# Causal scores in three tiles of PSUM instead of four, and one slice of the next latent query moved ahead of the values

## What is computed

```python
scores = einsum('bhsr,btr->bhst', q_lat, c_kv) + einsum('bhsd,btd->bhst', q_rope, k_rope[:, 0])
scores = scores / sqrt(DN + DR)
scores = where(tril(ones((s, s))), scores, finfo.min)      # s = 128, causal
probs  = softmax(scores, axis=-1)
out_lat = einsum('bhst,btr->bhsr', probs, c_kv)            # then w_uv and w_out per head
```

## Time and profile before

| | |
|---|---|
| time, median of 3 | 1919.72 us (1919.02 to 1920.83) |
| profiled execution, span | 1917.3 us |
| PE busy | 1909.2 us (100%), weight loads 1615.0 us (84%) |
| DVE, ACT, POOL busy | 1531.8 (80%), 1168.9 (61%), 1048.7 us (55%) |
| chain that ended last | PE 97%, DVE 2%, DMA 1% |
| DMA | 393.13 MB in 86473 packets, queue 58.0% of 16 engines |

### The profile page before, as it was taken

One profiled execution on the slowest core, in us unless ns is written; L12 is line 12 of the kernel. 1 busy time (PEld: TensorE's weight loads), 2 busy tenths in 40 slices (PEclk: granted clock), 3 DMA queues, 4 the chain that ended last, 5 costly groups with the idle time before them and its releaser, 6 DMA issues.

```text
span 1917.3 us, 32648 instructions
## 1 busy us (share of the span) xinstructions
PE 1909.2 (100%) x10048; PEld 1615.0 (84%) x10048; DVE 1531.8 (80%) x2655; ACT 1168.9 (61%) x2648; POOL 1048.7 (55%) x891
## 2 busy tenths in 40 slices
PE   9999999999999999999999999999999999999999
PEld 7888888888888888888888888888888877888887
DVE  6778888888888887877777777777878889996677
ACT  5456767676758575765555555555656668766441
POOL 5468777787869696865555556555565511000000
PEclk9999999999999999999999999999999999999999
DMA  9838474647474655588546264464628286466645
GB/s 361 333 105 317 133 260 130 253 125 263 122 266 138 231 171 199 195 319 328 181 151 233 77 230 132 158 207 140 217 82 302 91 285 250 198 220 245 229 152 176
DMA packets 86473, 393.13 MB, mean 205 GB/s; under 512 B 9472, under 2 KB 10240, under 8 KB 67328
## 3 DMA queue, kind: packets, MB, share of 16 engines
q1 hardware_dynamic: 86400, 392.21, 58.0%
HBM read 236.46 MB, written 155.71 MB: 205 GB/s over the span
## 4 chain that ended last, share of the span: by engine, by line
PE 97%; DVE 2%; DMA 1%; ACT 0%; issue 0%; DVEq 0%; POOL 0%; ACTq 0%; SPq 0%
PE at_out L1281 11%; PE at_out L1285 10%; PE at_out L1282 10%; PE at_qbank L55 7%; PE at_qbank L57 7%; PE at_qbank L56 7%; PE at_score L1244 6%; PE at_score L1235 3%; PE at_turned L1256 3%; PE at_qbank L1605 3%; PE at_score L1605 2%; PE at_out L1605 2%; PE at_value L56 2%; PE at_value L55 2%; PE at_value L57 2%; PE at_qbank L1608 2%
## 5 line engine op out<-in xcount | busy, mean ns | idle before, releaser
L2620 DVE TENSOR_TENSOR at_acc<-at_out,at_acc 128x512 f32<-128x512 f32 x640 | 438.9, 689 | 138.2 <-PE at_out L1285 136.2
L2266 POOL TENSOR_TENSOR at_acc<-at_stage,at_acc 128x512 f32<-128x512 f32 x256 | 332.3, 1298 | 184.1 <-ACT at_stage L1747 174.5
L1281 PE MATMUL at_out<-at_wvo,at_val_hi 128*128 128x512 f32 x896 | 365.3, 408 | 0.5 <-ACT at_stage L1747 0.2
L1285 PE MATMUL at_out<-at_wvo,at_val_lo 128*128 128x512 f32 x896 | 350.6, 391 | 0.0
L1282 PE MATMUL at_out<-at_wvo,at_val_hi 128*128 128x512 f32 x896 | 350.5, 391 | 0.0
L1747 ACT ACTIVATE at_stage<-at_out 128x512 f32<-128x512 f32 x256 | 153.0, 599 | 125.2 <-PE at_out L1285 112.9
L1787 ACT ACTIVATE at_pT_hi<-at_turned 128x512 fp32r<-128x512 f32 x128 | 76.4, 597 | 245.8 <-PE at_turned L1256 245.8
L2226 POOL TENSOR_TENSOR at_probs<-at_probs,at_row_stats 128x512 f32<-128x512 f32 x128 | 133.3, 1041 | 148.2 <-DVE at_row_stats L2582 148.2
L1781 ACT ACTIVATE at_probs<-at_probs,at_row_stats 128x128 f32<-128x128 f32 x512 | 197.7, 388 | 8.8 <-DVE at_row_stats L2577 8.8
L1285 PEld LDWEIGHTS at_out<-at_wvo,at_val_lo 128*128 128x128 f32 x896 | 168.4, 188 | 37.8
L1281 PEld LDWEIGHTS at_out<-at_wvo,at_val_hi 128*128 128x128 f32 x896 | 169.1, 189 | 31.1 <-DVE at_acc L2620 5.7
(11 more groups left out here) (313 smaller groups left out, 4772.3 us busy)
## 6 DMA issues: line engine op xcount, KB each, us to landing
parts_d<-at_rope_tmp SPq DMA_DIRECT2D x32, 1024.0 KB, 6.1
at_qrope<-parts_d SPq DMA_DIRECT2D x128, 256.0 KB, 5.3
wvo_d<-at_wvo SPq DMA_DIRECT2D x16, 2048.0 KB, 7.8
at_wvo<-wvo_d SPq DMA_DIRECT2D x16, 2048.0 KB, 8.1
ff_w_d<-ff_w SPq DMA_DIRECT2D x21, 1024.0 KB, 6.2
ff_w<-ff_w_d SPq DMA_DIRECT2D x21, 1024.0 KB, 4.8
ab_raw<-in_w_heads SPq DMA_DIRECT2D x32, 576.0 KB, 5.5
wvo_d<-at_wvo SPq DMA_DIRECT2D x16, 1024.0 KB, 9.8
```

Source lines behind the costliest of these rows:

```text
L1281: pe.matmul(out, hi, weight[:, 0], start=start, stop=False, skip_group_check=True)
L1285: pe.matmul(out, lo, weight[:, 0], start=False, stop=True, skip_group_check=True).then_inc(out_ready, 1)
L2266: pool.tensor_tensor(at, stage[group][z][:], at, ALU.add).then_inc(pool_added, 1)
L2620: dve.tensor_tensor(at, outb[FACTORS[name][2]][:], at, ALU.add).then_inc(added, 1)
```

## The change

For the 64 first queries of a square only the first 64 keys count, since the scores are causal. The changed kernel computes the 64 last queries of both heads of a batch in one tile (two heads x 64 queries on the partitions, 128 keys), one tile for each batch, and puts the first queries of both batches side by side in a third tile (64 keys for each batch). So there are two "late" tiles and one "early" one. The queries' layout in `qlat` and `qrope` becomes halves x heads x 64, so that the stationary operand of a tile lies together. The lower half of the partitions of `pT` for early queries is set to zero once. And `next_latent` issues its first slice ahead of `values`, not behind `product_6`. Some tiles get other homes in SBUF, and the order of the value blocks is changed to suit. The core of the diff:

```diff
             def relayout_in(m, c):
                 for j in range(4):
-                    sp.dma_start(as_f32(qrope[c][j * HALF:(j + 1) * HALF]), of[SLOT_OF_PART[j]]).then_inc(
-                        qrope_in[c], 16)
+                    for h in range(QUAD):
+                        to = as_f32(qrope[c][j * HALF:(j + 1) * HALF, h // PAIR, :, h % PAIR])
+                        sp.dma_start(to, of[SLOT_OF_PART[j]][:, h].rearrange("p (k q) -> p k q", q=HQ)).then_inc(
+                            qrope_in[c], 16)
...
                 for bl in range(2):
-                    cols = batch_cols(s, bl)
-                    for h in range(PAIR):
-                        pe.matmul(score[:, bl * PAIR + h], qrope[c][:, pair * PAIR + h, cols], rope_keys[:, :, cols],
-                                  start=h == 0, stop=False, skip_group_check=True)
+                    pe.matmul(score[:, bl], both_heads(qrope[c][:, pair, half_of(s, bl, 1)]), rope_keys[:, :, batch_cols(s, bl)],
+                              start=bl == 0, stop=False, skip_group_check=True)
+                for bl in range(2):
+                    pe.matmul(score[:, EARLY, :, early_keys(bl)], both_heads(qrope[c][:, pair, half_of(s, bl, 0)]),
+                              rope_keys[:, :, early_cols(s, bl)], start=bl == 0, stop=False, skip_group_check=True)
...
-                    cols = batch_cols(s, bl)
-                    for h in range(PAIR):
-                        ins = pe.matmul(score[:, bl * PAIR + h, 0], qlat[u % 2][:, h, cols], compressed[c][:, cols],
-                                        start=False, stop=True, skip_group_check=True)
+                    pe.matmul(score[:, bl, 0], both_heads(qlat[u % 2][:, half_of(s, bl, 1)]), compressed[c][:, batch_cols(s, bl)],
+                              start=False, stop=True, skip_group_check=True)
+                for bl in range(2):
+                    ins = pe.matmul(score[:, EARLY, 0, early_keys(bl)], both_heads(qlat[u % 2][:, half_of(s, bl, 0)]),
+                                    compressed[c][:, early_cols(s, bl)], start=False, stop=True, skip_group_check=True)
...
-                for j in range(PARTS):
-                    to = TURNED_AT[j]
-                    ins = pe.transpose(turned[:, to * SEQ:(to + 1) * SEQ], probs[s % 2][:, j, :], ident[:])
+                for to, tile in enumerate((1, 0, EARLY)):
+                    ins = pe.transpose(turned[:, to * SEQ:(to + 1) * SEQ], probs[s % 2][:, tile, :], ident[:])
...
                 product_2(m, s)
+                next_latent(m, s, end, kind, first, range(1))
                 if s + 1 < end:
                     values(m, s + 1, group_of(kind, s + 1))
...
                 product_6(m, s, kind)
-                next_latent(m, s, end, kind, first, range(QT - 1))
+                next_latent(m, s, end, kind, first, range(1, QT - 1))
...
                 act.wait_ge(turn_ready, STEPS * m + s + 1)
-                act.activation(pT_hi[:], turned[:], ACT.Copy).then_inc(pT_hi_done, 1)
+                act.activation(pT_hi[:, :, HQ:SEQ], late_turned, ACT.Copy).then_inc(pT_hi_done, 1)
+                for bl in range(2):
+                    act.activation(pT_hi[0:HQ, heads_at(bl), 0:HQ], early_turned[bl], ACT.Copy).then_inc(pT_hi_done, 1)
...
-                pool.tensor_tensor(probs[i][:], probs[i][:], rsum[i].unsqueeze(2).to_broadcast([P, PARTS, SEQ]),
+                pool.tensor_tensor(late, late, rsum[i][:, 0:2].unsqueeze(2).to_broadcast([P, 2, SEQ]), ALU.mult)
+                pool.tensor_tensor(early, early, rsum[i][:, 2:4].unsqueeze(2).to_broadcast([P, 2, HQ]),
                                    ALU.mult).then_inc(probs_ready, 1)
...
-                dve.wait_ge(pT_hi_done, STEPS * m + s + 1)
-                dve.tensor_tensor(pT_lo[:], turned[:], as_f32(pT_hi[:]), ALU.subtract).then_inc(pT_lo_done, 1)
+                dve.wait_ge(pT_hi_done, done + 2)
+                early(0)
+                dve.wait_ge(pT_hi_done, done + 3)
+                dve.tensor_tensor(pT_lo[:, :, HQ:SEQ], late_turned, as_f32(pT_hi[:, :, HQ:SEQ]), ALU.subtract)
+                early(1).then_inc(pT_lo_done, 1)
```

More of the change, by code:

```diff
@@ L136, in decoder, with high @@
     PRODUCTS, PLAIN = 7, 3
[L137 to L142, removed]
+    BLOCKS = PRODUCTS + 1
+    A21, A22, A11, A12, S2, S3, S4, S1 = (slice(j * SEQ, (j + 1) * SEQ) for j in range(BLOCKS))
+    DIRECT, SUMS = slice(SEQ, 4 * SEQ), slice(4 * SEQ, BLOCKS * SEQ)
+    A11_A12, S3_S4 = slice(A11.start, A12.stop), slice(S3.start, S4.stop)
+    HQ, HALVES = SEQ // 2, 2 * BPC
+    LATE, EARLY = slice(0, 2), 2
+    TILES = 3
+    def high(of):
+        return slice(of.start - SEQ, of.stop - SEQ)
     FACTORS = {"P1": (A11, "b11", 0), "P2": (A12, "b21", 1), "P6": (S2, "t2", 0), "P5": (S1, "t1", 0),
@@ L316, in decoder @@
         prep_turned = outb[1]
+        late_turned = turned[:, 0:2 * SEQ].rearrange("p (k q) -> p k q", q=HQ)
+        early_turned = [turned[bl * HQ:(bl + 1) * HQ, 2 * SEQ:3 * SEQ].rearrange("p (k q) -> p k q", q=HQ) for bl in range(2)]
         cr_turned, cr_out = qbank, [turned, value]
@@ L396, in batch_cols, with early_cols, half_of, both_heads @@
             return slice(b * SEQ, (b + 1) * SEQ)
+        def early_cols(s, bl):
+            return slice(batch_cols(s, bl).start, batch_cols(s, bl).start + HQ)
+        def half_of(s, bl, late):
+            return 2 * (2 * (s % 2) + bl) + late
+        def both_heads(of):
+            return of.rearrange("p h q -> p (h q)")
+        def early_keys(bl):
+            return slice(bl * HQ, (bl + 1) * HQ)
+        def heads_at(bl):
+            return slice(PAIR, 2 * PAIR) if bl == 0 else slice(0, PAIR)
         def place(s):
@@ L1278, in product @@
                 val, op, n = FACTORS[name]
-                out, hi, lo, weight = outb[n][:], val_hi[s % 2][:, val], val_lo[s % 2][:, val], wvo[pair][op]
+                out, hi, lo, weight = outb[n][:], val_hi[s % 2][:, high(val)], val_lo[s % 2][:, val], wvo[pair][op]
                 pe.matmul(out, hi, weight[:, 0], start=start, stop=False, skip_group_check=True)
@@ L1767, in latent @@
                 act.wait_ge(ql_mm, PAIR * (UNITS * m + u) + h + 1)
-                act.activation(qlat[u % 2][:, h, :], qbank[use % 2][:], ACT.Copy).then_inc(ql_out, 1)
+                act.activation(qlat[u % 2][:, :, h, :], qbank[use % 2][:].rearrange("p (k q) -> p k q", q=HQ),
+                               ACT.Copy).then_inc(ql_out, 1)
             def rope(m, c, halves=range(2)):
@@ L1780, in exps @@
                 for j in range(PARTS):
-                    ins = act.activation(probs[i][:, j, :], probs[i][:, j, :], ACT.Exp,
-                                         bias=nmax[i][:, j:j + 1], accum_out=sums[i][:, j:j + 1])
+                    rows = probs[i][:, j, :] if j < EARLY else probs[i][:, EARLY, early_keys(j - EARLY)]
+                    ins = act.activation(rows, rows, ACT.Exp, bias=nmax[i][:, j:j + 1], accum_out=sums[i][:, j:j + 1])
                 ins.then_inc(exp_ready, 1)
@@ L2606, in direct_values @@
                 dve.tensor_tensor(val_lo[s % 2][:, DIRECT], value[:, DIRECT],
[L2607 removed]
+                                  as_f32(val_hi[s % 2][:, high(DIRECT)]), ALU.subtract).then_inc(val_lo_done, 1)
             def add_product(m, s, group, name, bl, n):
@@ L3090, in constants @@
         "ident": np.eye(P, dtype=np.float32),
-        "mask": np.where(np.tril(np.ones((SEQ, SEQ), bool)), 0, MASKED).astype(np.float32),
+        "mask": np.concatenate([np.zeros((P, SEQ // 2)), np.tile(np.where(np.tril(np.ones((SEQ // 2, SEQ // 2), bool)), 0, MASKED),
+                                                                  (2, 1))], axis=1).astype(np.float32),
         "cos": np.tile(cos * root, (QUAD, 1)),
```

61 lines of the change are left out of this document (36 added, 25 removed).

## The result

The changed kernel takes 2016.56 us (median of 4 runs, 2015.39 to 2018.15), the kernel before 1920.28 beside it: ratio 1.0501, 95% interval 1.0486 to 1.0516. It is **96 us slower**, where 20 us faster was forecast.

A forecast was written before the change was run, and what follows sets the result against it. The prediction took PE to bound the kernel, the other engines and DMA having room on average. PE's steps gave -22 us and later waits +2, so 1919.7 becomes 1900 us, range 1891 to 1913.

The forecast's parts named there:

- The moved latent slice: Slice issued ahead of the values: its wait for a bank of `qbank` comes 1.4 us earlier, bank already drained; cost 0.
- PE, step by step: PE's transposes, rope scores and rests: smaller early tile saves 0.173 us a step, times 128 steps, -22 us.
- Case B: Rival on PE's early matmuls: columns count and not weight loads, -58 + 2, 1864 us; chance 0.07.
- What is late next: Work behind the values: probabilities reach the transposes later, 0.3 us for each of 7 waits for POOL, +2 us.
- SP and the DMAs: Relayouts of 16 DMAs, not 4: 7.2 us of issue; ACT waits up to 1.1 us for raw rope weights, absorbed; cost 0.
- C: Rival on the relayout's DMA pieces: somewhat slow, a relayout takes 10 us, +8 to +14, 1908 to 1914; chance 0.07.
- D: Rival on the relayout's DMA pieces: a relayout takes 15 us, PE stands 6.3 us in 6 quads, +38, 1938; chance 0.05.
- The chain from transposes to values: ACT's copies and DVE's subtraction ahead of the values: grows some 0.16 us, reserve grows from 0.76 to about 1.3 us.

The follow-up runs named there:

- g3: The changed kernel, slice moved, with DVE's middle full quads written out in place of a loop: 1993.2 us, ratio 1.0384.
- f1: The changed kernel with both latent slices back behind product 6 and DVE's quads 1 to 6 written out, not looped: 1919.5 us, ratio 1.0001.
- h2: g1 with the two first loads of `cr_x` issued ahead of the load of the last relayout: 1907.3 us, ratio 0.9932.
- e2: The kernel before with only the first latent slice moved ahead of the values, four tiles as before: 2001.1 us, ratio 1.0425.
- e3: The kernel before with the changed kernel's relayout, 16 DMAs with runs of 256 bytes in place of four of 2 KB: 1929.0 us, ratio 1.0045.
- e1: The changed kernel with both latent slices back behind product 6, nothing else undone: 1945.0 us, ratio 1.0128.
- e4: The kernel before with 40 waiting instructions more in DVE's loop over the full quads, 297 and not 257: 1962.6 us, ratio 1.0221.
- h1: The kernel before with e4's 40 instructions only in quad 0, ahead of DVE's loop, which keeps 257: 1920.1 us, ratio 0.9999.
- g4: The kernel before with 23 instructions more in DVE's loop over the full quads, 280 in all: 1966.6 us, ratio 1.0247.
- g1: f1 with SP issuing the raw rope weights and the switch's rope weights ahead of the relayout's 16 DMAs: 1912.0 us, ratio 0.9962.

## Why the prediction was wrong

The loss of 5.01% can be laid out along a row of kernels, each of which differs from its neighbour in one part (ratios to the kernel before that was measured beside each, times 1919.7 us): slice moved +73.5 (g3 less f1), DVE's loop +22.5 (changed less g3), SP's order with the small pieces +13.2 (f1 less h2), and the tiles on PE -13.1 (h2 less the kernel before). They add up to 96 us because neighbours cancel; that the parts stand by themselves is said by e2 (slice alone +82), e3 (pieces alone +9.6) and e1 (all but the slice +25).

- **"The moved latent slice ... Cost 0": the step that failed most.** It looked at one resource of the slice, the bank, and at the usual step. It left out what the slice had done where it was: it covered DVE's addition of product 6, which product 5 waits for. Two slices, 1.36 us, were enough; one is 0.44 us short (9.80 against 9.36 in e2). And "DVE and ACT finish the last within the first 1 to 2 us of a step" isn't so in steps 1 and 7 of a full quad, where three sums of 0.6 us stand behind the turning: 4.5 us. Measured, the slice cost 73.5 us and not 0.
- **DVE's instructions, loaded again in each turn: not in the prediction at all.** I counted DVE's instructions by their durations and not by their number. Forty more in a loop of 257 made it load its program again at each turn (e4: five packets and 6.2 to 7.9 us of pause), which no time of an instruction tells. The profile before had the sign to start from, no instruction packet from 315 to 750 us. 257 instructions ran without loading also from the start of e4's loop (h1), and 280 were loaded again in every turn (g4). Where between them the limit lies, and whether it is one of length alone, was not shown.
- **PE, step by step: the mechanism right, the size too large.** Forecast -0.173 us a step, measured -0.10 (9.36 to 9.26). Rope scores and transposes gave 0.15 of the 0.173. The rests gave nothing, as forecast: of the eight, the weight loads of the four with 64 columns start as far apart as those of the four with 128, 0.11 us (of the matmuls themselves one distance is 0.06), so columns don't set the pace there; the 0.11 us of a weight load fits. Case B is refuted. Its "nothing in the trace has 128 or fewer streamed columns with plain loads" was a wrong reading: the rests of the earlier trace rows have 128 columns and took 0.113 us beside 0.118 for 256. Some 0.04 us went again between product 1 and product 5, where fourteen matmuls of 512 columns stand 0.232 us apart in a later step of f1 and 0.230 before. I didn't test why.
- **"What is late next", +2 us: wrong sign, small.** POOL's wait ahead of the transposes went from 1.3 to 0.4 us.
- **SP and the DMAs, cost 0: too low by 13 us.** SP took 7.7 us for sixteen in most relayouts (7.2 forecast). The raw rope weights made ACT wait in f1 up to 1.2 us (0.54 in the row shown), near the "up to 1.1", but that was not absorbed: quads 2 to 6 take 92.0 to 92.4 us in f1 and 91.5 in g1. Two places were not looked at, the rope weights of the switch (2.6 us of waiting) and `cr_x` in quad 15 (70.2 us in g1, 64.5 in h2). C and D, priced by slow pieces, didn't occur: a DMA of the relayout landed 2.1 us behind its issue (median), so the issue set the pace.
- **The chain from transposes to values** had its reserve in the usual step, as forecast; with DVE's pause it was short by 2.8 us.

With the slice left in place the forecast would still have failed: e1 is 25 us slower than the kernel before. Only the tiles by themselves come out on the forecast side, at -13 us (h2) where -22 was worked out. The slice belonged among the rivals, on the slower side: 0.44 us of wait in some 113 steps is 50 us.

## What to carry to other kernels

When a piece of filler work is moved, price both ends: what it now waits for, step by step, and which wait it covered where it stood. Count the instructions of each engine's loop as well as their durations, those that only wait included; where the profile before shows no instruction packets inside a loop and the change makes it longer, the pause of a reload is a rival (4.1 to 8.6 us a turn in the kernels here). And where one queue issues everything, order it by who waits soonest.

## What was not expected of the hardware

- DVE's loop of 257 instructions ran without loading: no instruction packets from 315 to 750 us in the kernel before and in h1. So did the loop of 259 in the later quads of the changed kernel, with none from 1110 to 1570 us. With 280 (g4) and 297 (e4, e1, the changed kernel) each of the five turns has five packets, 0.04 MB in all. DVE then stands 4.1 to 4.7 us and 1.0 to 1.6 more a little later in the changed kernel and e1, 6.2 to 7.9 us at once in e4 and 7.1 to 8.6 in g4. Why it is longer there is open. Written out (f1), the same work shows no pause (none of 0.9 us or more without a cause from 300 to 800 us), though nine packets come from 305 to 774 us.
- While PE stood idle for 5.65 us in e4 its granted clock fell to 0.50, some 3 us in, and it was still 0.50 in the first 4 us of work (641 to 645 us; 0.42 us for a matmul and not 0.227). With it, 40 instructions that do nothing cost PE 7 to 10 us a turn (99.3 to 101.9 less 92.0). In the changed kernel a wait of 2.76 us left the clock at 1.00 (662 to 668 us).
